# Graph attention with a top-2 expert layer: more TensorE columns, a reordered hand-over, and one shared row per token

## The reference

```python
h  = layernorm(x)
h0 = gat_conv(h, W0, as0, ad0, b0, src, dst)              # 8 heads of 16
h1 = gat_conv(h, W1, as1, ad1, b1, src[dst], dst[dst])
x  = x + layernorm(concat(h0, h1) + h) * gamma + beta
y  = layernorm(x)
top_w, top_i = top_k(y @ Wg + bg, 2); top_w = softmax(top_w)
x  = x + sum over the two chosen experts e: top_w * (gelu(y @ W1[e] + b1[e]) @ W2[e] + b2[e])
```

## Time and profile before

| what | us |
|---|---|
| median of three runs | 3259.16 |
| the profiled execution | 3259.1 |
| its span, first to last instruction | 3257.1 |
| busy: DVE, POOL, PE, ACT | 2124.1, 2004.9, 1939.7, 1202.9 |

### The profile page before, as it was taken

The page is one execution under the profiler, slowest core; times in us unless marked ns, Lnnn a source line. Parts: engine busy times, 40 slices in busy tenths (PEclk is TensorE's granted clock), DMA queues, the critical chain, the costliest instruction groups (busy, mean ns, idle before and its releaser), DMA issues.

```text
span 3257.1 us, 33843 instructions
## 1 busy us (share of the span) xinstructions
PE 1939.7 (60%) x8606; PEld 1401.4 (43%) x8607; DVE 2124.1 (65%) x3771; ACT 1202.9 (37%) x2095; POOL 2004.9 (62%) x2011
## 2 busy tenths in 40 slices
PE   4600000006777677767776777601446999999998
PEld 2400000003343334334433343301445999999997
DVE  8536767667788878887888778876863333333332
ACT  3313444443333433343334333433452333333332
POOL 4677777777777777777777777776762222222222
PEclk8755555557888888878888888855557999999999
DMA  9735447844444344444444444355673222222222
GB/s 288 169 56 145 152 164 156 220 122 124 149 127 123 122 154 123 122 123 153 124 122 122 151 127 122 124 201 178 207 242 91 36 36 36 37 36 37 36 37 29
DMA packets 221064, 400.68 MB, mean 123 GB/s; under 512 B 78416, under 2 KB 172772, under 8 KB 213802
## 3 DMA queue, kind: packets, MB, share of 16 engines
q1 hardware_dynamic: 142057, 247.16, 22.8%
q0 software_dynamic: 77792, 151.99, 21.2%
q10 hardware_dynamic: 1120, 0.52, 0.1%
HBM read 207.94 MB, written 191.63 MB: 123 GB/s over the span
## 4 chain that ended last, share of the span: by engine, by line
POOL 48%; PE 25%; issue 16%; DVE 6%; DMA 2%; ACT 2%; DVEq 1%; SPq 0%; POOLq 0%; ACTq 0%
POOL AR L743 44%; PE ps L1175 11%; PE ps L1181 11%; POOL AR L731 1%; DVE AR L1264 1%; POOL adstart L715 1%; POOL AR L776 1%; ACT AR L1017 1%; PE ps L1166 1%; DMA out<-AR,idb 1%; PE ps L1155 1%; ACT AR L1003 1%; PE ps L1143 1%; PE ps L1072 0%; POOL AR L783 0%
## 5 line engine op out<-in xcount | busy, mean ns | idle before, releaser
L743 POOL DMA_INDIRECT AR<-tables,idx x1505 | 1421.5, 945 | 458.7 <-issue 458.7
L1101 PE MATMUL ps<-AR 128*128 128x408 f32 x2584 | 983.5, 546 | 775.0 <-DVE AR L1488 775.0
L1101 PEld LDWEIGHTS ps<-AR 128*128 128x128 f32 x2584 | 529.0, 207 | 1229.2 <-issue 813.7
L824 POOL DMA_INDIRECT out<-AR,idb x105 | 186.1, 1772 | 593.2 <-issue 558.4
L1420 DVE TENSOR_TENSOR_SCAN AR<-ps,AR 128x512 f32<-128x512 f32 (+2 forms) x495 | 519.9, 1125 | 4.0
L930 ACT ACTIVATE ps<-AR 128x512 f32<-128x512 f32 (+1 forms) x440 | 255.8, 589 | 470.7 <-DVE AR L1420 470.7
L937 ACT COPY AR<-AR 128x1984 f32<-128x1984 f32 (+3 forms) x110 | 423.7, 3899 | 0.7 <-DVE AR L1420 0.7
L1175 PEld LDWEIGHTS ps<-AR 128*128 128x128 f32 x3360 | 393.1, 193 | 6.5 <-DVE AR L1848 1.2
L1175 PE MATMUL ps<-AR 128*128 128x128 f32 x3360 | 393.7, 276 | 0.8 <-DVE AR L1848 0.8
L1414 DVE TENSOR_TENSOR AR<-AR,ps 128x3968 f32<-128x3968 f32 (+3 forms) x55 | 371.1, 6746 | 0.3
L1848 DVE COPY AR<-AR 128x1024 f32 x210 | 150.8, 719 | 205.8 <-PE ps L1175 204.4
(11 more groups left out here) (318 smaller groups left out, 1996.1 us busy)
## 6 DMA issues: line engine op xcount, KB each, us to landing
state<-AR SPq DMA_DIRECT2D x52, 2232.0 KB, 9.5
AR<-tables,idx POOLq DMA_INDIRECT x1585, 2.6
AR<-in_L_ffn_W SPq DMA_DIRECT2D x16, 1024.0 KB, 9.9
AR<-placed SPq DMA_DIRECT2D x105, 129.0 KB, 2.0
AR<-adstart SPq DMA_DIRECT2D x53, 248.0 KB, 4.0
adstart<-zero SPq DMA_DIRECT2D x26, 496.0 KB, 4.8
tables<-AR SPq DMA_DIRECT2D x49, 136.0 KB, 2.5
hbd<-eb2b SPq DMA_DIRECT2D x7, 896.0 KB, 9.1
```

What stands on the lines that cost most here:

```text
L743: pool.indirect_dma_start(out=G[s][:, j, 0:ROWT], out_offset=None, in_=table_rows, in_offset=bass.IndirectOffsetOnAxis(ap=idx[:, s, j:j + ...
L824: pool.indirect_dma_start(out=out, out_offset=bass.IndirectOffsetOnAxis(ap=idb[:, s, :], axis=0), in_=ys[:, s, :], in_offset=None, bounds_ ...
L1101: mm = T.matmul(ps[c][:, 0:w], onehot[c][:, a, :], table_cols[:, a * w:(a + 1) * w], start=(a == 0), stop=(a == LEV - 1))
```

## The change

TensorE takes two columns in the 43 batches 9 to 51, the last batch among them. For this the second normalisation and the storing of X move one batch forward (batches 1 to 7), the table is loaded in batch 6, and the codes are written in batch 6; `run_maxima(0)` and `run_sums(0)` now run ahead of batch 1. `column_codes` moves into `hT4`. In the last stage the fix row is gathered after three groups of `last_states2` rather than four, corrected earlier on DVE, and one more group is gathered while it is stored. ACT writes each normalised row once; both scatters send the same row, which now carries the token's number, both weights, and the number of its first expert. `pr` has four buffers. In the expert stage `rows_of` picks the weight: it reads the tile's expert, compares it with the first expert of each row, and selects.

```diff
-ROWP = D + 2
+ROWP = D + 4
-PEEL = 9
+PEEL = 8
-PE0, PE1 = 13, 51
+PE0, PE1 = 9, 52
+TABLE_AT = 6
...
                 def fetch(s, b):
+                    if b == PE0:
+                        sp.wait_ge(lists_stored, 32)
...
-                    if 2 <= b < PEEL:
-                        g = b - 2
-                        sp.wait_ge(biased_ready, g + 1)
+                    if 1 <= b < PEEL:
+                        g = b - 1
+                        sp.wait_ge(biased_ready, 2 * (g + 1))
                         sp.dma_start(hbd[g], ...)
+                        sp.dma_start(xkept[g], ...)
+                    if b == TABLE_AT:
+                        sp.wait_ge(x_rows_stored, 16 * TABLE_AT)
...
+                        sp.dma_start(table_cols[:, 0:NT * ROWT]...)
-                    if b == FIX + 2:
+                    if b == FIX + 1:
                         sp.wait_ge(codes_ready, 1)
                         sp.dma_start(codes.rearrange("c p -> p c"), src_code[:, :])
...
-            for j in range(J):
+            for j in range(fetched_columns(NB - 1)):
...
-            for n in range(4):
+            pool.wait_ge(columns_ready, PEC * (PE1 - PE0))
+            for n in range(3):
                 last_states2(n)
             for s in range(NS):
                 pool.wait_ge(batch_stored[s], 16 * (BS if s else BS + 1))
             gather_fix_rows(1, 0)
+            last_states2(3)
             store_fix_rows(1, 0)
+            last_states2(4)
             pool.wait_ge(fix_rows_stored, 32)
-            for n in range(3):
+            for n in range(4):
                 last_states1(n)
-            last_states2(4)
-            last_states1(3)
             last_states2(5)
             last_states2(6)
...
-                                                in_=pr[n % 2][:, k, t, :], ...).then_inc(tokens_placed[n % 2], 16)
+                                                in_=pr[n % 4][:, t, :], ...).then_inc(tokens_placed[n % 4], 16)
...
-                if g >= 2:
-                    act.wait_ge(tokens_placed[g % 2], 16 * 2 * GRP * (g // 2))
+                if g >= 4:
+                    act.wait_ge(tokens_placed[g % 4], 16 * 2 * GRP)
...
                 turned_copy(GRP - 1)
-                for t in range(GRP):
-                    last = row_of(1, t)
-                last.then_inc(group_normalised, 1)
...
+            take_columns(b)
-            dve.wait_ge(conv2_gathered, 16 * (J1 + J - CUT))
+            dve.wait_ge(conv2_gathered, 16 * (J1 + fetched_columns(b) - CUT))
...
             run_sums(1)
+            fix_maxima(1)
             combine(1, 1)
+            fix_sums(1)
             shares(1, 2)
+            shares(1, 3)
             combine(1, 2)
-            fix_maxima(1)
-            shares(1, 3)
-            fix_sums(1)
             combine(1, 3)
...
-            def rows_of(s):
-
+            def rows_of(s, e):
+
+                V.tensor_copy(expert_now[:, s, :], e8[:, bass.ds(e, 1)])
                 V.tensor_copy(idb[:, s, :], xs[:, s, D:D + 1])
-                V.tensor_copy(wb[:, s, :], xs[:, s, D + 1:D + 2]).then_inc(row_ids_copied, 1)
+                dd()
+                V.scalar_tensor_tensor(both_w[:, s, 0:1], xs[:, s, D + 3:D + 4], expert_now[:, s, :], xs[:, s, D + 1:D + 2], ALU.is_equal, ALU.mult)
+                V.scalar_tensor_tensor(both_w[:, s, 1:2], xs[:, s, D + 3:D + 4], expert_now[:, s, :], xs[:, s, D + 2:D + 3], ALU.not_equal, ALU.mult).then_inc(row_ids_copied, 1)
+                dd()
+                V.tensor_tensor(wb[:, s, :], both_w[:, s, 0:1], both_w[:, s, 1:2], ALU.add)
...
                     hold(dve, 4, tile_loaded[1 - s], (i + (1 + s)) * 16)
                     if not (first and s == 0):
                         hold(dve, 4, answer_added, t * 16)
-                    rows_of(1 - s)
+                    rows_of(1 - s, expert_of(i * 2 + (s + 1)))
                 e = expert_of(t)
                 dve.wait_ge(answer_product_ready, t + 1)
```

More of the change, by code:

```diff
@@ L134, in build @@
         at += PEC * LEV * P
-        column_codes = AR[:, at:at + NS * PEC * P].rearrange("p (s e) -> p s e", s=NS)
-        assert at + NS * PEC * P <= FB and LEV * TPL >= NT
+        assert at <= FB and LEV * TPL >= NT and NS * PEC * P <= 4 * D
         zero = sb("zero", [P, 1024])
@@ L204, in build @@
         wb = sb("wb", [P, 2, 1])
+        both_w = sb("both_w", [P, 2, 2])
+        expert_now = sb("expert_now", [P, 2, 1])
         ps = [ctx.enter_context(nc.psum_tensor(f"ps{i}", [P, 512], F32)) for i in range(8)]
@@ L307, in build @@
         first_rows_ready = sem("first_rows_ready")
-        tokens_placed = [sem("tokens_placed_a"), sem("tokens_placed_b")]
+        tokens_placed = [sem(f"tokens_placed{i}") for i in range(4)]
         expert_weights_loaded = sem("expert_weights_loaded")
@@ L444, in build @@
                                                                      hT4.rearrange("p s d -> p (s d)")[:, 0:GRP * ROWS])]
[L445 to L448, removed]
+        pr = [AR[:, a:a + GRP * ROWP].rearrange("p (t r) -> p t r", r=ROWP) for a in range(FB, FB + 4 * GRP * ROWP, GRP * ROWP)]
+        assert FB + 4 * GRP * ROWP <= AW
         own_score = sb("own_score", [P, NT, 16])
@@ L644, in _ @@
                 sp.wait_ge(x_rows_stored, 32 * NG)
-                sp.wait_ge(group_normalised, 2 * NG)
+                for i in range(3):
+                    sp.wait_ge(tokens_placed[i], 16 * 2 * GRP * (2 if i + 4 < NG - 1 else 1))
+                sp.wait_ge(first_rows_ready, 4 * NG)
                 down_in(6)
-                sp.wait_ge(tokens_placed[1], 16 * 2 * GRP * (NG // 2))
                 down_in(7)
@@ L652, in _ @@
                     sp.dma_start(placed[bass.ds(r, P), :], padrow[:, :]).then_inc(pads_stored, 16)
-                sp.wait_ge(tokens_placed[0], 16 * 2 * GRP * (NG - NG // 2))
+                for i in range(4):
+                    sp.wait_ge(tokens_placed[i], 16 * 2 * GRP * (2 if i + 4 < NG else 1))
                 sp.wait_ge(pads_stored, 16 * NEX + 16)
@@ L959, in whole_batch @@
             def whole_batch(s, i, b, more=True):
-                if isinstance(b, int) and b >= 2 and b < PEEL:
-                    normalise_again(b - 2)
+                if 1 <= b < PEEL:
+                    normalise_again(b - 1)
                 batch_weights(b + 2, J, False)
@@ L968, in whole_batch @@
                 copy_back(b + 2, s, J)
[L969 removed]
+                if b == 0:
                     carry_exps(0)
@@ L988, in deviations @@
             def deviations(g, q):
-                act.wait_ge(group_variance_ready, 2 * g + q + 1)
-                S.activation(group_scale[:, 0, :], group_mv[:, :, 1], ACT.Sqrt).then_inc(group_deviation_ready, 1)
+                act.wait_ge(variances_ready, NG + 2 * g + q + 1)
+                S.activation(group_scale[:, 0, :], group_mv[:, :, 1], ACT.Sqrt).then_inc(deviations_ready, 1)
                 act.wait_ge(group_scales_ready, 2 * g + q + 1)
@@ L995, in _ @@
             share_exps(1, 1)
-            share_exps(1, 2)
             fix_exps(1)
-            share_exps(1, 3)
+            for g in range(2, 4):
+                share_exps(1, g)
             share_exps(0, 0)
@@ L1013, in _, with row_of @@
                 deviations(g, 1)
-                if g >= 2:
-                    act.wait_ge(tokens_placed[g % 2], 16 * 2 * GRP * (g // 2))
-                def row_of(k, t):
-                    return S.activation(pr[g % 2][:, k, t, 0:D], X[:, g * GRP + t, :], ACT.Identity, bias=group_scale[:, 2, t:t + 1], scale=group_scale[:, 1, t:t + 1])
+                if g >= 4:
+                    act.wait_ge(tokens_placed[g % 4], 16 * 2 * GRP)
+                def row_of(t):
+                    return S.activation(pr[g % 4][:, t, 0:D], X[:, g * GRP + t, :], ACT.Identity, bias=group_scale[:, 2, t:t + 1], scale=group_scale[:, 1, t:t + 1])
                 def turned_copy(t):
@@ L1025, in _ @@
                     for q in range(t, min(t + 2, GRP)):
-                        last = row_of(0, q)
+                        last = row_of(q)
                     last.then_inc(first_rows_ready, 1)
@@ L1611, in _ @@
             dd()
-            for b in range(2, NB - 1):
+            for b in range(1, NB - 1):
                 if b < PEEL:
-                    add_biases(b - 2)
+                    add_biases(b - 1)
                 whole_batch(b % NS, b // NS, b, CUT + 1 if b == NB - 2 else L)
@@ L1889, in _ @@
             dve.wait_ge(expert_weights_loaded, 32 * NEX)
-            for s in range(2):
-                dve.wait_ge(tokens_placed[s], 16 * 2 * GRP * ((NG + 1 - s) // 2))
+            for i in range(4):
+                dve.wait_ge(tokens_placed[i], 16 * 2 * GRP * (2 if i + 4 < NG else 1))
             for h in range(2):
@@ L1901, in _ @@
             dve.wait_ge(tile_loaded[0], 16)
-            rows_of(0)
+            rows_of(0, expert_of(0))
             for s in range(2):
```

38 lines of the change are left out of this document (16 added, 22 removed).

## The result

| | before | after |
|---|---|---|
| median, us (4 runs each) | 3258.34 | 3362.86 |
| lowest and highest | 3257.4, 3260.79 | 3362.65, 3364.67 |
| span of the profiled execution | 3257.1 | 3361.1 |
| first bias add of the experts starts | 2493.5 | 2475.4 |
| one expert tile, mean of 104 periods | 7.245 | 8.419 |

The changed kernel is slower by a ratio of 1.0321 (95% interval 1.0303 to 1.0339). The forecast was 3356 us with a range of 3310 to 3400. Medians of the experiments are over fast runs; one run of E7 took 3846.35 us at a granted clock of 0.614, against 0.80 in its others, and is left out.

The account below looks back on a forecast made before the run. POOL's gather issue bounds the batches, hand-overs the last stage, PE the experts, with a loop 0.22 us below it. 3259.1 - 20.5 (ahead of the experts) + 118 (longer loop) = 3356.6; forecast 3356 us, range 3310 to 3400.

Parts of the forecast that it names:

- What bounds each stretch: POOL's issue bounds the edge batches, hand-overs the last stage; in the experts the loop has 0.22 us slack a tile.
- the loop: Experts: bias add, product, POOL's add, landing, `rows_of`, register load, next bias add; 7.03 us a tile, becoming 8.38.
- The load: Expert stage, `rows_of`: the new `expert_of` register load stands behind the landed answer and adds about 0.70 us a tile.
- The selection: Expert stage, rest of the `rows_of` extension: address, drains and two scalar_tensor_tensors; total with the load 1.35 us a tile.
- The columns: Edge batches: ten gathers fewer save 12.5 us on POOL; DVE leaves the batches about 9.8 us earlier.
- The moves: Early batches: normalisation, `run_maxima`, `run_sums`, table and codes moved forward cost nothing; failed cover means some 7 us once or twice.
- The fix rows: Last stage: store at 2191, first states at about 2201.5, DVE starts 11.5 us sooner, containing the batches' 9.8; bounds 9 and 14.
- The shared row: Last stage: fewer ACT instructions and four buffers cut DVE's waits for square roots by 9.0 us; bounds 4 and 11.
- The added work is hidden: Rival, experts: the extension of `rows_of` costs under 0.22 us of loop time, giving 3238.6 us; chance 8%.
- Both weight copies ahead of POOL: Rival, experts: back-to-back weight copies hold POOL's instruction; 9.6 us a tile, 245 us more, 3484 us; chance 5%.
- PE's clock: Rival, experts: PE's pauses lower its granted clock to 1.2 GHz, giving near 3990 us; chance 2%.
- The front gives nothing: Rival, ahead of the experts: a late store or table load eats the saving, giving 3377 us; chance 9%.

Follow-up runs that it names:

- E7: E5 with ACT's seven row copies a group put back, writing to memory nothing reads, four buffers kept; 3245.66 us.
- E4: The kernel before with one more, unused register load behind the wait for the answer; 7.567 us a tile.
- E2: The changed kernel with only the new register load moved ahead of the wait for the answer; 7.765 us a tile.
- E10: The same kernel as E2, run again on the same chip; 7.737 us a tile.
- E6: E5 with ten columns back on POOL, so TensorE takes columns only in batches 13 to 50; 3245.48 us.
- E8: E5 with the old order around the fix row on POOL, DVE and ACT; 3238.02 us.
- E5: The changed kernel with both register loads, comparison and selection ahead of the wait, only the row-number copy behind; 3237.91 us.

## Why the prediction was right

**What bounds each stretch** held. POOL's issue bounds the batches at 1.25 us a gather, and a chain of hand-overs the last stage. In the experts the loop was 0.24 us below PE (E4), and took over.

**The load, 0.70 us.** E2 and E10 show 0.65 and 0.68 in the period, E4 0.66 between the landing and the copy. The step's reason, that a load behind a wait cannot start during it, is shown by E2: moved ahead, it costs nothing that can be seen.

**The selection, 1.35 - 0.70 = 0.65 us.** It is larger. From the landing to the copy of the row numbers the changed kernel takes 0.95 us on average and the kernel before 0.13; from there to the bias add it takes 1.62, and 0.93 in E4, which has the old `rows_of` and waits for PE before only 4 bias adds. That is 0.82 + 0.69 = 1.51 us added, of which 0.67 are the load (in E2 the copy comes 0.29 behind the landing) and 0.84 the rest. One mis-sized term shows in the timeline: the two scalar_tensor_tensors take 0.22 and 0.21 us at 128x1, where 0.17 was taken from the 128x7 row. Against it the landing came 0.09 us sooner (3.94 us behind the start of POOL's instruction, 4.02 before), for which the step had no term, and the loop before is 6.08 + 0.93 = 7.01 where 7.03 was taken. 7.01 + 1.51 - 0.09 = 8.43: 0.19 too little and 0.14 too much nearly cancel, and that 8.38 came so close to 8.42 is in part luck.

**The columns, 12.5 us on POOL.** The gathers end 11.6 us sooner in the changed kernel (2159.1 and 2147.5), though they start 0.4 later (238.3 against 237.9); 0.5 of the 12.5 us stay unexplained. "DVE leaves the batches about 9.8 us earlier" came to 2164.22 - 2156.00 = 8.2 by its last scan of the batches (L1383). The last `take_columns` is not the reason: it does fill the wait of 2.20 us, as costed (from L1373 to L1383 are 2.63 us before and 2.68 after). The loss is there one batch sooner. Before:

```profile
2124.64 0.57 DVE L1383 TENSOR_TENSOR AR<-AR,ps 128x248 f32<-128x248 f32 x1 [9.44 <-DMA AR<-tables,idx]
```

and after:

```profile
2116.26 0.57 DVE L1383 TENSOR_TENSOR AR<-AR,ps 128x248 f32<-128x248 f32 x1 [3.91 <-DMA AR<-tables,idx]
```

These are 8.4 us, where the eight gathers saved by then are 10.0: POOL's last gather of that batch starts only 9.0 us sooner (2119.4 and 2110.4), about the 0.4 and 0.5 above, and the rows come 0.6 later behind it. The step had no term for the loss behind DVE either: 7.6 us reach the end (E6).

**The moves, nothing.** The first scan of batch 1 starts 3.2 us late (319.9 instead of 316.7) and the next one 3.9, but that of batch 3 is level again (397.3 and 397.5), so the cover held.

**The fix rows.** The step said 2201.5 for the first states and 2191 for the store. The store came at 2191.97, the states at 2203.97:

```profile
2191.97 1.01 POOL L762 DMA_INDIRECT state<-fix_row,fix_index  x1 [6.52 <-DVE sml L1594]
...
2203.97 1.85 POOL L784 DMA_INDIRECT AR<-state,node_index  x1 [0.30 <-issue]
...
2215.40 0.22 DVE L1659 TENSOR_TENSOR share_of<-AR,bare 128x56 f32<-128x56 f32 x1 [10.38 <-DMA AR<-state,node_index]
```

DVE starts 2223.80 - 2215.40 = 8.4 us sooner, not 11.5, below the lower bound of 9. Of the 3.1 us missing 1.0 lie ahead of the store (2191.97 for 2191), 1.5 in the seven gathers behind it (12.0 us from store to states, where 2201.5 - 2191 = 10.5 were taken), and the rest behind the first gather of states, which itself takes 1.85 us here and 0.97 in the earlier trace rows. E8 shows that the new order is worth 0.1 us and not 11.5 - 9.8 = 1.7.

**The shared row, 9.0 us.** The waits fell by 10.3 (12.5 - 2.2), in the bounds. E7 gives the activations 7.8 us at the end.

Together: E6, E7 and E8 return 7.6 + 7.8 + 0.1 = 15.5 of the 18.1 us, and the 2.6 us of the scatters would make 18.1 (that last term is a difference of waits and not a run, and starts of single executions differ by about 1 us, so the sum is no closer than that). The forecast was 20.5. The forecast time misses by 2.4 us here (20.5 - 18.1) and by 4.1 in the experts (122.1 - 118), both the same way.

**The rivals.** "The added work is hidden" gave 3238.6 us; it was refuted (E2), but is near what E5 measured (3237.91), where the work does lie beside the wait. "Both weight copies ahead of POOL" would have held POOL's instruction until both end; a copy runs when it starts in 59 of 105 tiles, but the hold stays small, and its mean is 1701 ns, below the 1772 of the kernel before. PE's clock stayed at 0.99. "The front gives nothing" fell with the 18.1 us.

## What to carry to other kernels

DVE issues in order, so a wait is a line: what stands behind it runs when the event has come, even if it needs nothing of it (a register load cost 0.65 us behind the wait and nothing ahead of it, E2). Sort what follows a wait into what needs the event and what doesn't, register loads and their drains included; here that move alone was worth 125 of 3363 us, with no work less. An engine busy 39% may still be the bound, if a loop of hand-overs runs through it: add up the loop from one timeline and compare it with the period before adding anything to it. Read the period from the body of the loop too: a mean over all tiles had 0.024 us in it that came from the last nine. And an edit that brings an event forward is worth only what then stands first behind it: the fix row was stored 8 us sooner, and nothing came of it.

## What was not expected of the hardware

Seven indirect gathers right behind the scattering store took 2203.00 - 2191.39 = 11.6 us in E5, where seven at 1.25 take 8.75; three lasted 1.76 to 1.86 us instead of 0.94. The store is not what holds them. Each begins 0.05 to 0.15 us behind the start of a tensor_tensor of DVE with both inputs in the fast memory, and ends 0.82 us behind its end. Two of the three:

```profile
2194.69 1.09 DVE L1695 TENSOR_TENSOR AR<-AR,zero 128x896 f32<-128x896 f32 x1
...
2200.79 1.09 DVE L1695 TENSOR_TENSOR AR<-AR,hT 128x896 f32<-128x896 f32 x1
```

2194.69 + 1.09 + 0.82 = 2196.60, where POOL's gather of 2194.74 ends, and 2200.79 + 1.09 + 0.82 = 2202.70, where that of 2200.84 ends. Of the 21 gathers of states in E5 that took over 1.05 us, 20 end 0.81 to 0.86 us behind such an instruction; of nine that began while DVE read the accumulator memory (L1414, L1420, L1476) none was held. In the kernel before 23 of 28 that began within such a tensor_tensor were held; why the other five were not stays open, and no run moved either side.

A scalar_tensor_tensor on 128x1 whose scalar is a value per partition in memory takes 0.22 us, more than one on 128x7 with a constant in the earlier trace rows (0.168) and as much as one on 128x56 with constants (L1679, 0.218). So its length does not go by the number of elements alone; that the operand from memory is what costs is likely, but was not tried.
